# Q and K: the rounded and the remaining part of a projection, made by ScalarE and GpSimd in place of ScalarE and VectorE

## The chip, the core and the metric

The kernel runs on one core of one Trainium2 chip. The metric is the device time of one launch in microseconds (us); of the kernel before it is 1079.29 us, the median of 3 runs (1078.25 to 1079.56). TensorE multiplies, VectorE, ScalarE and GpSimd do elementwise work, SyncE issues the transfers. In the profile they are PE (PEld is its weight load), DVE, ACT, POOL and SP.

## What is computed

One transformer layer, post-LayerNorm, on 16 sequences of 512 tokens with 256 features, all in float32. 16 heads of 16 features attend in blocks of 128 tokens to the block before, their own and the block after; the feed-forward part has weights that are quantised to -1, 0 and 1.

```python
qkv = (x @ Wqkv + bqkv)                  # split into q, k, v; 16 heads of 16
scores = einsum(q_block, k_window) / 16  # window of 3 blocks, |kpos - qpos| <= 128
attn = softmax(scores)
x = layernorm(x + (attn @ v) @ Wout + bout)
h = relu(x @ quantise(W1).T + b1)
x = layernorm(x + h @ quantise(W2).T + b2)
```

## The kernel before

One row is one of the 16 sequences. The program is a software pipeline over rows, with a step for each row from -2 to 16. In a step, attention runs for row b, everything behind the attention (output projection, LayerNorms, feed-forward) for row b-1, and the projections of Q, K and V for row b+1. A step has four quarters v = 0 to 3, one for each quad of heads. The list `SIDE` names the side work of each quarter in order. In quarter 1 it is `("qk", 0), ("x1", 0), ("x1", 1), "nmt", "pv", ("x1", 2), "ut", ("x1", 3), "x1t", ("qk", 1), ("f1", 0)`; quarter 2 starts with `("f1", 1), "vp"`. Into this side work `WOVEN` puts 12 units per quarter of scores (L549, then an exp on ScalarE, L895) and of maximum scores (L567, then a masked row maximum on VectorE, L1061). Every engine walks the same list in its own program order and waits on semaphores.

Products are made from TensorE's rounded type fp32r. A float32 value is therefore kept as two tiles: hi is the value rounded, lo is what is left of it. Q and K of a row come as four tiles of 128x512, `QK[0]` to `QK[3]`; `("qk", 0)` makes `QK[0]` and `QK[1]`, `("qk", 1)` the other two. For each, TensorE fills a pair of the four shared PSUM banks `PG`. ScalarE then writes hi with the bias added (L919, `s_qkh`), and VectorE reads the same bank again, adds the bias and subtracts hi (L1088, `s_qkl`). After that the pair is free: the next user of the pair waits for `reader[k]`, here `s_qkl`. The same two steps on the same two engines make the parts of other products, `hid_hi` (L976) and `hid_lo` (L1147) of the feed-forward among them.

What stands around Q and K in quarter 1, by engine:

- TensorE: `("qk", 0)`, then the turned maxima (L631), `pv` (L641), `ut` on the pair that `("qk", 0)` had (two warming products L521 ahead of it, then L654, which needs ScalarE's copy `u`, L946), `x1t` (four warming products L521, then L612, which needs all four parts of `x1`), `("qk", 1)`, `f1` 0, `f1` 1 on the pair that `("qk", 1)` had, and `vp` on the pair of `f1` 0, for which `hid_lo` of `f1` 0 must be done.
- ScalarE: `qk_hi` twice, `x1` 0 and 1 (L963), `neg_maxT` (L938), `u` (L946), two exps, `x1` 2 and 3, the turned `x1` (L969), six exps, `qk_hi` twice, two exps, `hid_hi` twice.
- VectorE: row maxima throughout, `qk_lo` twice after units 0 and 1, the reciprocals and products of `ut` (L1095, L1102), the turned `x1`, `qk_lo` twice after unit 9, maxima 10 and 11, then `neg_max` (L1069 and L1072, two small instructions on 128x16 elements), then `hid_lo` twice.
- GpSimd: zeroes the masked probabilities after the exps 5 and 11 (L1285 and L1289), makes the small values of LayerNorm (L1351 to L1357), adds a bias to `x1` (L1360). It has no access to PSUM in this program; all that it reads is in SBUF.
- SyncE copies the parts into the stacked operands `SQ` and `SK` (`stack`, L449): first the four transfers of hi, then the two of lo, which wait for `s_qkl`; behind them in its queue stand the transfer of the maxima (L489) and later stacks. Stack 0 of the next row is first used by unit 0 of quarter 2.

Of the kernel before, what the change touches and what calls it, by code (L numbers as in the profile page):

```python
# [21 lines left out]
F32 = mybir.dt.float32  # L22
F32R = mybir.dt.float32r
ALU = mybir.AluOpType
ACT = mybir.ActivationFunctionType
# [197 lines left out]
def postln_layer(nc, xT, x, wqkv, bqk, bv, wout, bout, w1T, b1, w2T, b2, out):  # L223
    ctx = ExitStack()
    with ctx:
# [3 lines left out]
        def sem(name):  # L229
            return ctx.enter_context(nc.semaphore(name))  # L230
# [101 lines left out]
        s_qkf = sem("qk_full")  # L332
        s_qkh = sem("qk_hi_done")
        s_qkl = sem("qk_lo_done")
        s_vf = sem("v_full")
        s_v = sem("v_next_done")
        s_va = sem("v_aug_done")
# [77 lines left out]
        def _(sp):  # L415
# [17 lines left out]
            def stack(r, v, first):  # L433


                c, ih = v // 2, v % 2
                if not first:
                    sp.wait_ge(s_stf, 12 * (4 * r - 4 + v) + 12)
                half = slice(64 * ih, 64 * ih + 64)
                heads = slice(4 * ih, 4 * ih + 4)  # L440
                for part, done in ((0, s_qkh), (1, s_qkl)):
                    sp.wait_ge(done, 4 * r + 2 * c + 2)
                    for dst, j, terms in ((SQ, 2 * c, (0, 1, 0)), (SK, 2 * c + 1, (0, 0, 1))):
                        if first and v == 0 and dst is SK:
                            continue
                        for t in range(3):
                            if terms[t] == part:
                                rows = slice(64 * c + 16 * t, 64 * c + 16 * t + 16)
                                sp.dma_start(dst[rows, heads, :].bitcast(F32), QK[j][part][half, :].bitcast(F32)) \  # L449
                                    .then_inc(s_stk[v], 16)  # L450
# [51 lines left out]
        def _(pe):  # L502
# [117 lines left out]
            def side_work(v, step, b, dr, vq, at, passed):  # L620
# [37 lines left out]
                elif name == "qk":  # L658
# [8 lines left out]
                    def tokens(z, kc):  # L667
# [1 line left out]

                    in_halves(out, [three_terms(slice(0, S), lambda a, kc: weights(a, kc, j), tokens)  # L670
                                    for j in (2 * c, 2 * c + 1)], s_qkf, passed)
                    reader[k] = [(s_qkl, 4, 2 * c + 2, dr)]
                elif name in ("vp", "op"):
                    left, right, col = (XT, WQKV, 2 * D) if name == "vp" else (OT, WOUT, 0)
                    if first:
# [176 lines left out]
        def _(act):  # L852
# [10 lines left out]

            def first_k_stack():

                for part, done in ((0, s_qkh), (1, s_qkl)):
                    act.wait_ge(done, 2)
                    for t, term in enumerate((0, 0, 1)):
                        if term == part:
                            act.dma_start(SK[16 * t:16 * t + 16, 0:4, :].bitcast(F32),  # L870
                                          QK[1][part][LOWER, :].bitcast(F32)).then_inc(s_stk[0], 16)
# [26 lines left out]
            def side_work(v, step, b, dr, vq, at):  # L898
# [11 lines left out]
                elif name == "qk":  # L910
# [7 lines left out]
                    for i, j in enumerate((2 * c, 2 * c + 1)):  # L918
                        act.activation(QK[j][0][:, :], PG[:, 2 * k + i, :], ACT.Identity, bias=BQK[:, j:j + 1]) \  # L919
                            .then_inc(s_qkh, 1)  # L920
                    if first and c == 0:
                        first_k_stack()
                        weight_sums()
                    elif first:
                        act.wait_ge(s_b1, 64)
                        act.activation(B1R[:, :], B1RAW, ACT.Identity).then_inc(s_b1h, 1)
# [99 lines left out]
        def _(dve):  # L1026
# [48 lines left out]
            def side_work(v, step, b, dr, vq, at):  # L1075
# [4 lines left out]
                if step == ("xs", 1) and first:  # L1080
                    dve.wait_ge(s_xh, 2)
                    dve.tensor_tensor(XT[1][:, :, :], XRAW[:, :, :], XT[0][:, :, :].bitcast(F32),
                                      ALU.subtract).then_inc(s_xl, 1)
                elif name == "qk":
                    c = step[1]
                    for i, j in enumerate((2 * c, 2 * c + 1)):
                        dve.wait_ge(s_qkh, 4 * r + j + 1)
                        dve.scalar_tensor_tensor(QK[j][1][:, :], PG[:, 2 * k + i, :], BQK[:, j:j + 1],  # L1088
                                                 QK[j][0][:, :].bitcast(F32), ALU.add, ALU.subtract) \
                            .then_inc(s_qkl, 1)  # L1090
                elif name == "ut":
                    q = 4 * r + vq
                    dve.wait_ge(s_utf, 2 * q + 2)
# [162 lines left out]
        def _(pool):  # L1256
# [76 lines left out]
            def side_work(v, step, b, dr, vq, at):  # L1333
                name = name_of(step)
                r = b + dr
                first = at is not None and at + dr == 0
                if step == ("xs", 1) and not first:
                    pool.wait_ge(s_xh, 2 * r + 2)
                    pool.tensor_tensor(XT[1][:, :, :], XRAW[:, :, :], XT[0][:, :, :].bitcast(F32),
                                       ALU.subtract).then_inc(s_xl, 1)  # L1340
                elif name == "xr":
                    pool.wait_ge(s_xr, 16 * r + 16)
                    if first:
                        pool.wait_ge(s_b2, 32)
                    pool.tensor_tensor(Y[:, :, :], Y[:, :, :], BOUT[:, None, :].to_broadcast([P, TB, D]),
                                       ALU.add).then_inc(s_xrb, 1)
                elif name == "ln1" and step[1] % 2 == 1:
                    hf = step[1] // 2
                    two = slice(2 * hf, 2 * hf + 2)
                    pool.wait_ge(s_mv1, 4 * r + 2 * hf + 2)  # L1350
                    pool.tensor_scalar(VE[:, two], MV1[:, two, 1], 1.0, EPS, ALU.mult, ALU.add).then_inc(s_ve, 1)  # L1351
                    pool.tensor_scalar(NEG1[:, two], MV1[:, two, 0], -1.0, None, ALU.mult).then_inc(s_neg, 1)
                    pool.wait_ge(s_ve, 4 * r + 1 + hf)
                    pool.tensor_tensor(RS1[:, two], VE[:, two], HALF[:, two], ALU.pow).then_inc(s_rs1, 1)
                    pool.wait_ge(s_neg, 2 * r + hf + 1)
                    pool.wait_ge(s_rs1, 2 * r + hf + 1)
                    pool.tensor_tensor(NMR1[:, two], NEG1[:, two], RS1[:, two], ALU.mult).then_inc(s_nmr, 1)  # L1357
                elif name == "x1t":
                    pool.wait_ge(s_x1tf, 2 * r + 2)
                    pool.tensor_tensor(X1[:, :, :], X1[:, :, :], B2[:, None, :].to_broadcast([P, TB, D]),  # L1360
                                       ALU.add).then_inc(s_x1b, 1)
                elif name == "ln2" and step[1] % 2 == 1:
                    h = step[1] // 2
                    two = slice(h, h + 3, 2)
                    pool.wait_ge(s_mv2, 4 * r + 2 * h + 2)
                    pool.tensor_scalar(VE[:, two], MV2[:, two, 1], 1.0, EPS, ALU.mult, ALU.add).then_inc(s_ve, 1)
                    pool.wait_ge(s_ve, 4 * r + 3 + h)
                    pool.tensor_tensor(RS2[:, two], VE[:, two], HALF[:, two], ALU.pow).then_inc(s_rs2, 1)
                    pool.wait_ge(s_rs2, 2 * r + h + 1)
                    for t in (h, h + 2):  # L1370
                        pool.tensor_scalar(X1[:, t, :], X1[:, t, :], MV2[:, t, 0:1], RS2[:, t:t + 1],  # L1371
                                           ALU.subtract, ALU.mult).then_inc(s_o, 1)
# [82 lines left out]
```

## Time and profile before

| | kernel before |
|---|---|
| median of 3 runs | 1079.29 us (1078.25 to 1079.56) |
| the profiled execution: time | 1080.47 us |
| its span | 1078.7 us |
| PE busy | 996.8 us (92%) |
| DVE busy | 845.2 us (78%) |
| ACT busy | 620.2 us (57%) |
| POOL busy | 570.2 us (53%) |
| mean granted clock of TensorE | 0.969 of full |

The span is the profiled stretch from the first to the last instruction. The time of the same execution is 1.8 us longer, the launch around it. A busy share is an average over the whole span; what a step costs is read from the timeline of a row, where one sees which wait ends last. A wait is printed in square brackets behind the instruction that it held up, with the engine that ended it.

### The profile page before, as it was taken

Reading aid. Unit: us, or ns where it says so; the run is one execution under the profiler, and the core shown is the slowest. Engines: PE = TensorE matmul, PEld = TensorE weight load, DVE = VectorE, ACT = ScalarE, POOL = GpSimd, SP = SyncE. Lnnn points to the kernel's source line nnn. Section 1 sums busy time; section 2 is a strip of 40 time slices with the busy share of each in tenths; the row PEclk is TensorE's granted clock in tenths of the full one; section 3 lists DMA queues with packets and bytes.
Section 4 is the critical chain, followed back from the end, with each engine's and each line's share of the span. In section 5 each row is a group of like instructions: output and inputs, shape, how many; then the busy total and the mean of one; then the engine's idle time right before and its main releaser. Section 6 shows DMA issues by size and latency. Waiting matters only on the chain.

```text
span 1078.7 us, 29877 instructions
## 1 busy us (share of the span) xinstructions
PE 996.8 (92%) x11270; PEld 782.0 (72%) x11270; DVE 845.2 (78%) x2966; ACT 620.2 (57%) x1273; POOL 570.2 (53%) x913
## 2 busy tenths in 40 slices
PE   6898999999999999999999999999999999999897
PEld 5675777777777777777767777786777778687677
DVE  3775888879788887978888787988878798887535
ACT  4244665746566574756657474765747475564632
POOL 3975356374655537465554646454464645445352
PEclk8577999999999999999999999999999999999999
DMA  9554336546354545626454652645365364435000
GB/s 222 64 82 72 57 57 95 81 74 94 55 91 66 96 70 81 99 43 97 66 96 63 94 87 49 100 65 96 56 100 80 57 96 68 73 52 81 22 21 20
DMA packets 57023, 81.90 MB, mean 76 GB/s; under 512 B 7712, under 2 KB 27696, under 8 KB 56880
## 3 DMA queue, kind: packets, MB, share of 16 engines
q1 hardware_dynamic: 56640, 79.60, 46.8%
q8 instruction: 90, 1.47, 0.7%
q10 hardware_dynamic: 240, 0.39, 0.3%
q14 instruction: 53, 0.43, 0.2%
HBM read 20.20 MB, written 8.39 MB: 26 GB/s over the span
## 4 chain that ended last, share of the span: by engine, by line
PE 61%; DVE 13%; ACT 12%; issue 6%; POOL 4%; DMA 2%; SPq 1%; DVEq 0%; POOLq 0%; ACTq 0%
PE shared L592 26%; PE shared L641 11%; PE st L549 8%; PE mx L567 6%; DVE mx L1061 6%; ACT probs L895 4%; PE shared L521 2%; ACT x L963 2%; ACT u L946 2%; DVE hid_lo L1147 2%; PE shared L654 2%; ACT oT_x1T_hi L969 2%; PE shared L612 1%; POOL probs L1285 1%; POOL probs L1289 1%
## 5 line engine op out<-in xcount | busy, mean ns | idle before, releaser
L1061 DVE CUSTOM_DVE_ANT_0 mx<-mx,band 128x384 f32<-128x384 f32 (+1 forms) x1024 | 478.9, 518 | 150.5 <-PE mx L567 145.4
L895 ACT ACTIVATE probs<-st 128x384 f32<-128x384 f32 (+1 forms) x768 | 365.1, 526 | 169.8 <-PE st L549 168.1
L1285 POOL TENSOR_SCALAR_AFFINE_SELECT probs<-probs 128x512 f32<-128x512 f32 (+1 forms) x256 | 127.8, 524 | 407.0 <-ACT probs L895 407.0
L567 PE MATMUL mx<-k_stack,q_stack 48*128 48x384 f32 (+1 forms) x1024 | 271.7, 347 | 8.5 <-DMA q_stack<-qk_lo 4.9
L549 PE MATMUL st<-q_stack,k_stack 50*128 50x384 f32 (+1 forms) x1024 | 245.1, 334 | 7.8 <-ACT probs L895 3.8
L549 PEld LDWEIGHTS st<-q_stack,k_stack 50*128 50x128 f32 x1024 | 167.7, 189 | 58.9 <-issue 29.8
L567 PEld LDWEIGHTS mx<-k_stack,q_stack 48*128 48x128 f32 x1024 | 171.8, 193 | 31.1 <-DVE rmax L1061 19.2
L641 PE MATMUL shared<-probs,v_aug 128*32 128x384 f32 (+1 forms) x2048 | 164.2, 444 | 9.4 <-POOL probs L1289 7.2
L1061 DVE DVE_READ_ACCUMULATOR2_ANT rmax<- 128x1 f32 x1024 | 144.9, 141 | 0.0
L592 PE MATMUL shared<-w2q,hid_hi 64*128 64x256 f32 x960 | 137.0, 289 | 0.0
L641 PEld LDWEIGHTS shared<-probs,v_aug 128*32 128x32 f32 x2048 | 90.5, 111 | 55.8 <-issue 17.7
L592 PE MATMUL shared<-w2q,hid_lo 64*128 64x256 f32 x960 | 129.2, 278 | 0.0
L1289 POOL TENSOR_SCALAR_AFFINE_SELECT probs<-probs 128x512 f32<-128x512 f32 (+1 forms) x256 | 127.7, 523 | 0.0
L592 PEld LDWEIGHTS shared<-w2q,hid_lo 64*128 64x128 f32 x960 | 114.9, 185 | 0.0
L592 PEld LDWEIGHTS shared<-w2q,hid_hi 64*128 64x128 f32 x960 | 113.3, 185 | 0.4
L592 PE MATMUL shared<-oT_x1T_hi,w1q 64*128 64x512 f32 x480 | 104.0, 398 | 0.0
L592 PE MATMUL shared<-oT_x1T_lo,w1q 64*128 64x512 f32 x480 | 102.4, 394 | 0.0
L946 ACT ACTIVATE u<-shared 128x512 f32<-128x512 f32 x64 | 37.9, 593 | 102.1 <-PE shared L641 102.0
L521 PE MATMUL shared<-wqkv_hi 64*128 64x512 f32 x516 | 86.6, 417 | 3.9 <-DVE qk_lo L1088 3.8
L1147 DVE SCALAR_TENSOR_TENSOR hid_lo<-shared,hid_hi 128x512 fp32r<-128x512 f32 x120 | 77.0, 682 | 16.1 <-ACT hid_hi L976 16.1
L1371 POOL TENSOR_SCALAR x<-x,ln_mv,ln_rstd 128x256 f32<-128x256 f32 x60 | 73.5, 1230 | 3.2
L976 ACT ACTIVATE hid_hi<-shared 128x512 fp32r<-128x512 f32 x120 | 65.2, 596 | 13.9 <-PE shared L592 12.7
(165 smaller groups left out, 1935.7 us busy)
## 6 DMA issues: line engine op xcount, KB each, us to landing
q_stack<-qk_hi SPq DMA_DIRECT2D x128, 128.0 KB, 4.0
k_stack<-qk_hi SPq DMA_DIRECT2D x126, 128.0 KB, 4.9
x_raw<-in_xT SPq DMA_DIRECT2D x16, 512.0 KB, 6.0
q_stack<-qk_lo SPq DMA_DIRECT2D x64, 128.0 KB, 5.6
y<-in_x SPq DMA_DIRECT2D x16, 512.0 KB, 6.3
out<-x SPq DMA_DIRECT2D x32, 256.0 KB, 2.4
k_stack<-qk_lo SPq DMA_DIRECT2D x63, 128.0 KB, 5.8
probs<-in_w2T SPq DMA_DIRECT2D x1, 1024.0 KB, 7.5
```

What stands on the lines that cost most here:

```text
L521: pe.matmul(out[i][:, 0:width], WQKV[0][rows, 0, 0:P], WQKV[0][rows, 1, 0:width], start=True, stop=True)
L549: mm = pe.matmul(PST[i % N_SCORE][:, col:col + n], SK[rows, hd, W * m:W * m + W], SQ[rows, hd, q0:q0 + n], start=True, stop=True)
L567: mm = pe.matmul(PMX[i % N_MAX][:, col:col + n], SQ[rows, hd, W * m:W * m + W], SK[rows, hd, k0:k0 + n], start=True, stop=True)
L592: mm = pe.matmul(out[k][:, cols], lhs(rows), rhs(rows), start=(swap == 0 and n == 0 and bias is None), stop=(swap == 1 and n == count - 1) ...
L641: mm = pe.matmul(out[0][32 * g:32 * g + 32, q0:q0 + width], VAUG[:, vq, m, g, :], PR[:, vq % 2, g // 2, lo:lo + width], start=(m == 0), st ...
L895: act.activation(PR[:, v % 2, g // 2, lo:lo + n], PST[i % N_SCORE][:, 0:n], ACT.Exp, scale=SCALE) \
L976: act.activation(HID[0][:, f, :], PG[:, 2 * k + i, :], ACT.Relu).then_inc(s_hh, 1)
L1061: mx = dve.tensor_tensor_reduce(ps, ps, band, 1.0, -3e38, ALU.add, ALU.max, RMAX[:, g, m:m + 1])
L1147: dve.scalar_tensor_tensor(HID[1][:, f, :], PG[:, 2 * k + i, :], 0.0, HID[0][:, f, :].bitcast(F32), ALU.max, ALU.subtract).then_inc(s_hl, 1)
L1285: pool.affine_select(out=pr_before, in_=pr_before, compare_op=ALU.is_ge, fill=0.0, base=0, pattern=[[0, n], [1, W]], channel_multiplier=-1)
L1289: last = pool.affine_select(out=pr_after, in_=pr_after, compare_op=ALU.is_ge, fill=0.0, base=0, pattern=[[0, n], [-1, W]], channel_multipl ...
L1371: pool.tensor_scalar(X1[:, t, :], X1[:, t, :], MV2[:, t, 0:1], RS2[:, t:t + 1], ALU.subtract, ALU.mult).then_inc(s_o, 1)
```

## The change

For every row but the first, ScalarE copies each bank of Q and K twice. The first copy is hi as before. The second writes the full value with its bias into the lo tile, as plain float32 (`s_qkw`, new). GpSimd then subtracts hi from it in place, SBUF to SBUF, and raises `s_qkl`. VectorE no longer touches Q and K of these rows. The pair of banks is free when ScalarE's second copies are done. The first row keeps the old way, with a semaphore of its own (`s_qkl0`). On GpSimd the new step stands behind the masks that are woven into the `qk` step; in quarter 1 that is ahead of the mask of exp 11.

```diff
--- before.py
+++ after.py
@@ -332,6 +332,8 @@
         s_qkf = sem("qk_full")
         s_qkh = sem("qk_hi_done")
         s_qkl = sem("qk_lo_done")
+        s_qkl0 = sem("qk_lo_done_in_first_row")
+        s_qkw = sem("qk_copied")
         s_vf = sem("v_full")
         s_v = sem("v_next_done")
         s_va = sem("v_aug_done")
@@ -438,8 +440,13 @@
                     sp.wait_ge(s_stf, 12 * (4 * r - 4 + v) + 12)
                 half = slice(64 * ih, 64 * ih + 64)
                 heads = slice(4 * ih, 4 * ih + 4)
-                for part, done in ((0, s_qkh), (1, s_qkl)):
-                    sp.wait_ge(done, 4 * r + 2 * c + 2)
+                for part in range(2):
+                    if part == 0:
+                        sp.wait_ge(s_qkh, 4 * r + 2 * c + 2)
+                    elif first:
+                        sp.wait_ge(s_qkl0, 2 * c + 2)
+                    else:
+                        sp.wait_ge(s_qkl, 4 * r - 4 + 2 * c + 2)
                     for dst, j, terms in ((SQ, 2 * c, (0, 1, 0)), (SK, 2 * c + 1, (0, 0, 1))):
                         if first and v == 0 and dst is SK:
                             continue
@@ -669,7 +676,7 @@
 
                     in_halves(out, [three_terms(slice(0, S), lambda a, kc: weights(a, kc, j), tokens)
                                     for j in (2 * c, 2 * c + 1)], s_qkf, passed)
-                    reader[k] = [(s_qkl, 4, 2 * c + 2, dr)]
+                    reader[k] = [(s_qkl0, 0, 2 * c + 2, dr)] if first else [(s_qkw, 4, 2 * c - 2, dr)]
                 elif name in ("vp", "op"):
                     left, right, col = (XT, WQKV, 2 * D) if name == "vp" else (OT, WOUT, 0)
                     if first:
@@ -863,7 +870,7 @@
 
             def first_k_stack():
 
-                for part, done in ((0, s_qkh), (1, s_qkl)):
+                for part, done in ((0, s_qkh), (1, s_qkl0)):
                     act.wait_ge(done, 2)
                     for t, term in enumerate((0, 0, 1)):
                         if term == part:
@@ -918,6 +925,9 @@
                     for i, j in enumerate((2 * c, 2 * c + 1)):
                         act.activation(QK[j][0][:, :], PG[:, 2 * k + i, :], ACT.Identity, bias=BQK[:, j:j + 1]) \
                             .then_inc(s_qkh, 1)
+                        if not first:
+                            act.activation(QK[j][1][:, :].bitcast(F32), PG[:, 2 * k + i, :], ACT.Identity,
+                                           bias=BQK[:, j:j + 1]).then_inc(s_qkw, 1)
                     if first and c == 0:
                         first_k_stack()
                         weight_sums()
@@ -1081,13 +1091,13 @@
                     dve.wait_ge(s_xh, 2)
                     dve.tensor_tensor(XT[1][:, :, :], XRAW[:, :, :], XT[0][:, :, :].bitcast(F32),
                                       ALU.subtract).then_inc(s_xl, 1)
-                elif name == "qk":
+                elif name == "qk" and first:
                     c = step[1]
                     for i, j in enumerate((2 * c, 2 * c + 1)):
                         dve.wait_ge(s_qkh, 4 * r + j + 1)
                         dve.scalar_tensor_tensor(QK[j][1][:, :], PG[:, 2 * k + i, :], BQK[:, j:j + 1],
                                                  QK[j][0][:, :].bitcast(F32), ALU.add, ALU.subtract) \
-                            .then_inc(s_qkl, 1)
+                            .then_inc(s_qkl0, 1)
                 elif name == "ut":
                     q = 4 * r + vq
                     dve.wait_ge(s_utf, 2 * q + 2)
@@ -1338,6 +1348,11 @@
                     pool.wait_ge(s_xh, 2 * r + 2)
                     pool.tensor_tensor(XT[1][:, :, :], XRAW[:, :, :], XT[0][:, :, :].bitcast(F32),
                                        ALU.subtract).then_inc(s_xl, 1)
+                elif name == "qk" and not first:
+                    for j in (2 * step[1], 2 * step[1] + 1):
+                        pool.wait_ge(s_qkw, 4 * r - 4 + j + 1)
+                        pool.tensor_tensor(QK[j][1][:, :], QK[j][1][:, :].bitcast(F32), QK[j][0][:, :].bitcast(F32),
+                                           ALU.subtract).then_inc(s_qkl, 1)
                 elif name == "xr":
                     pool.wait_ge(s_xr, 16 * r + 16)
                     if first:
```

## Rows read from the trace of the kernel before

**Rows 1.** The page: busy time by engine; then the chain that ended last.
```profile
PE 996.8 (92%) x11270; PEld 782.0 (72%) x11270; DVE 845.2 (78%) x2966; ACT 620.2 (57%) x1273; POOL 570.2 (53%) x913
PE 61%; DVE 13%; ACT 12%; issue 6%; POOL 4%; DMA 2%; SPq 1%; DVEq 0%; POOLq 0%; ACTq 0%
```
**Rows 2.** Windows: stretch, its length, busy PE PEld DVE ACT POOL, clock, DMA.
```profile
40.00:80.00 40.00, 35.81 (x216) 26.09 (x218) 28.68 (x109) 16.67 (x35) 33.17 (x37) 0.68 0.72 93
...
120.00:182.40 62.40, 58.88 (x708) 46.29 (x706) 51.71 (x184) 38.29 (x80) 33.33 (x55) 1.00 0.48 71
...
931.20:993.60 62.40, 58.84 (x710) 46.38 (x708) 51.88 (x185) 37.26 (x79) 30.95 (x54) 1.00 0.46 71
```
**Rows 3.** Timeline of ScalarE from 436 us: start, length, line, operands, count, [idle <-releaser].
```profile
435.86 1.27 ACT L919 ACTIVATE qk_hi<-shared,bqk 128x512 fp32r<-128x512 f32 x2 [0.79 <-PE shared L592]
437.49 1.09 ACT L963 ACTIVATE x<-y,ln_neg_mean_rstd,ln_rstd 128x256 f32<-128x256 f32 x2 [0.36 <-POOL ln_neg_mean_rstd L1357]
...
439.97 1.07 ACT L963 ACTIVATE x<-y,ln_neg_mean_rstd,ln_rstd 128x256 f32<-128x256 f32 x2
```
**Rows 4.** Timeline of TensorE in the same stretch, instructions that waited.
```profile
439.27 0.51 PE L521 MATMUL shared<-wqkv_hi 64*128 64x512 f32 x2 [0.37 <-DVE qk_lo L1088]
...
441.10 0.28 PE L612 MATMUL shared<-identity,x 64*128 64x64 f32 x2 [0.21 <-ACT x L963]
```
**Rows 5.** Timeline of VectorE in the same stretch.
```profile
437.81 1.41 DVE L1088 SCALAR_TENSOR_TENSOR qk_lo<-shared,bqk,qk_hi 128x512 fp32r<-128x512 f32 x2
```
**Rows 6.** Timeline of ScalarE around the second Q and K step.
```profile
446.65 1.27 ACT L919 ACTIVATE qk_hi<-shared,bqk 128x512 fp32r<-128x512 f32 x2
447.80 1.00 ACT L895 ACTIVATE probs<-st 128x384 f32<-128x384 f32 x2
448.96 1.09 ACT L976 ACTIVATE hid_hi<-shared 128x512 fp32r<-128x512 f32 x2 [0.17 <-PE shared L592]
```
**Rows 7.** Timeline of VectorE around the second Q and K step.
```profile
448.71 0.56 DVE L1061 CUSTOM_DVE_ANT_0 mx<-mx,band 128x384 f32<-128x384 f32 x1
...
450.12 0.36 DVE L1069 TENSOR_SCALAR neg_max<-rmax 128x16 fp32r<-128x16 f32 x1
450.51 0.32 DVE L1072 SCALAR_TENSOR_TENSOR neg_max<-rmax,neg_max 128x16 f32<-128x16 f32 x1
450.76 1.27 DVE L1147 SCALAR_TENSOR_TENSOR hid_lo<-shared,hid_hi 128x512 fp32r<-128x512 f32 x2
```
**Rows 8.** Timeline of TensorE's weight loads there, those that waited.
```profile
448.84 0.18 PEld L579 LDWEIGHTS shared<-ones,b_rows 64*128 64x128 f32 x2 [0.39 <-DVE qk_lo L1088]
452.09 0.19 PEld L592 LDWEIGHTS shared<-wqkv_hi,xT_hi 64*128 64x128 f32 x2 [0.97 <-DVE hid_lo L1147]
```
**Rows 9.** Timeline of GpSimd in quarter 1.
```profile
438.85 0.20 POOL L1357 TENSOR_TENSOR ln_neg_mean_rstd<-ln_neg_mean,ln_rstd 128x2 f32<-128x2 f32 x1
...
446.10 2.39 POOL L1360 TENSOR_TENSOR x<-x,b_rep 128x1024 f32<-128x1024 f32 x1
448.87 1.00 POOL L1285 TENSOR_SCALAR_AFFINE_SELECT probs<-probs 128x512 f32<-128x512 f32 x2 [0.38 <-ACT probs L895]
```
**Rows 10.** Timeline of GpSimd beside the neg_max pair of Rows 7.
```profile
450.40 0.41 POOL L1289 TENSOR_SCALAR_AFFINE_SELECT probs<-probs 128x256 f32<-128x256 f32 x1
```
**Rows 11.** The first neg_max of the run, and GpSimd beside it.
```profile
35.67 1.27 POOL L1303 TENSOR_TENSOR w2q<-w2q,oT_x1T_lo 128x512 fp32r<-128x512 f32 x1
36.93 1.56 POOL L1299 TENSOR_SCALAR oT_x1T_lo<-probs,abs_sums_thresholds 128x512 fp32r<-128x512 f32 x1
36.26 0.71 DVE L1069 TENSOR_SCALAR neg_max<-rmax 128x16 fp32r<-128x16 f32 x1
37.01 0.63 DVE L1072 SCALAR_TENSOR_TENSOR neg_max<-rmax,neg_max 128x16 f32<-128x16 f32 x1
```
**Rows 12.** Timeline of SyncE, stack 0; then the page's DMA issues (median us to landing).
```profile
440.36 0.61 SPq L449 DMA_DIRECT2D k_stack<-qk_lo  x1
...
k_stack<-qk_lo SPq DMA_DIRECT2D x63, 128.0 KB, 5.8
```

## The prediction

> **What bounds the kernel now.** I read the page first: TensorE is busy 92% of the span, VectorE 78%, ScalarE 57%, GpSimd 53%, but the chain that ended last is only 61% TensorE; 13% of it is VectorE and 12% ScalarE [rows 1]. So TensorE sets the pace with handovers in between, and what the change is worth depends on who ends which handover, not on the shares. The windows show 14 rows alike from 120 to 993.6 us: 62.4 us each, of which TensorE is busy 58.8 to 58.9, at a granted clock of 1.00, that is the 2.4 GHz level [rows 2]. The change touches quarter 1 of every row, so the timeline of one such row (the step from 432 us) decides, and 14 times its shift is the answer.
>
> In that quarter there are two places. In the first (436 to 441 us) ScalarE works almost without a gap: `qk_hi` twice, 0.36 us of waiting, then `x1`, `neg_maxT`, `u`, exps, `x1` to 441.04 [rows 3]; TensorE then waits for the last `x1`, until 441.10 [rows 4]. Its wait for `qk_lo` just before (0.37 us [rows 4]) is followed by warming products and is not the last handover. In the second place VectorE works in one piece from 448.71 to 452.03: maxima 10 and 11, `neg_max`, `hid_lo` [rows 7], and TensorE's next projection waits for that `hid_lo` until 452.09, its weight load for 0.97 us; shortly before, it waited 0.39 us for `qk_lo` [rows 8].
>
> **The change, part by part.** It removes 2 VectorE instructions per step, 1.41 us as a pair [rows 5], and adds 2 ScalarE copies and 2 GpSimd subtractions. Over 30 steps (15 rows, 2 each) VectorE loses 42 us of work.
>
> A ScalarE copy: two `qk_hi` take 446.65 to 447.80, where the next instruction starts [rows 6], so 0.575 us each in a sequence. Between there and the whole 0.69 of the last one (1.27 less 0.575 [rows 3]) I take 0.575, because neighbours overlap in the same way here. Two more: +1.15 us.
>
> The Trainium skill ("ScalarE: Activation LUTs", What ACT_TABLE_LOAD costs) gives an ACTIVATE with a bias operand 280 ns + 0.833 ns per element less about 93 ns of overlap, an estimate of 0.614 us for 512 elements; the two would be 1.23 us. The row is shorter and decides.
>
> First place. Four copies run from 435.86 to 438.16 and `x1` 0 starts there, not at 437.49 [rows 3]: +0.67. GpSimd's LayerNorm values were ready by 437.49, so ScalarE itself is late next. All that stands behind `x1` 0 in its queue follows: `u`, two exps, and the last `x1`, whose end moves from 441.04 to 441.71. The pair of banks is free at about 438.4 instead of 439.2, but then `ut` waits for `u`, and TensorE's wait for the last `x1` still ends last. Shift of TensorE behind this place: +0.67. VectorE's 1.41 us buy nothing here.
>
> GpSimd in the first place: it is free at 439.05, and until 446.10 it has one mask to do, four instructions in some 2 us [rows 9]. Two subtractions of 128x512, bounded by the 1.27 us of a subtraction of that size [rows 11] and half of the 2.39 us of 1024 columns, 1.20 [rows 9]; I take 1.27, the same size: 439.05 to 441.6. The lo transfers of stack 0, the later of which was issued at 440.36 and takes 5.8 us to land [rows 12], go at about 442.3 and land at 448.1; their first user stands just behind the first half of `f1` 1, at about 451. Behind them in SyncE's queue the transfer of the maxima moves from about 441.0 to 442.9, for the same user. Cost nothing; the cover is 3 us.
>
> Second place. ScalarE arrives 0.67 late (447.32), makes four copies (to 449.62), then the two exps (1.16 to the next start, less the 0.17 of waiting [rows 6]: 0.99, to 450.61), then `hid_hi`, whose first half ends at about 451.2 and whose second at 451.70. `hid_lo` could then run 451.25 to 452.5. TensorE gets the pair for `f1` 1 at 449.85 instead of 448.84 (+1.01), and comes to the projection at 451.12 (452.09 less 0.97 [rows 8]) + 1.01 = 452.13, ahead of 452.5. By ScalarE alone the projection starts at 452.6: +0.5 a row.
>
> But VectorE has `neg_max` ahead of `hid_lo`, and there GpSimd matters. The two small instructions take 0.36 and 0.32 us at 450.12 and 450.51 [rows 7]. The second ends at 450.83, GpSimd's mask instruction beside it at 450.81 [rows 10]. At the start of the run L1069 takes 0.71, from 36.26 to 36.97, while a GpSimd subtraction of 128x512 ends at 36.94; the instruction after it, L1072, takes 0.63 beside a GpSimd instruction with one tensor input, and ends before it [rows 11]. I read this as: while a GpSimd instruction runs, at least one that subtracts, `neg_max` waits for its end.
>
> The Trainium skill ("SBUF — State Buffer", Who interferes with whom) says that a VectorE instruction in a 2-port mode, or with two SBUF inputs while GpSimd reads SBUF, and a GpSimd instruction exclude each other for a whole instruction. By that rule, which speaks against this change, the trace mostly agrees; the 0.63 us of L1072 it does not explain.
>
> In the changed kernel GpSimd ends the bias of `x1` (446.10 + 2.39 [rows 9]) 0.67 later, at 449.16, and its subtractions run 449.16 to 450.43 and, the second copy of `QK[3]` being done at 449.73, 450.39 to 451.66. Maxima 10 and 11 no longer stand behind `qk_lo` but behind TensorE; they start at about 448.4 and `neg_max` is issued at about 449.85. Its first half then ends with the first subtraction (450.46), its second with the second (451.7), and `hid_lo` runs to about 452.89 in place of 452.03: +0.86 a row. The mask of exp 11 goes from 448.87 [rows 9] to 451.7; its `pv` comes ten us later, so this is free.
>
> **The sum.** 14 rows x 0.86 = 12.0 us. The fifteenth row (63 to 76 us) has no LayerNorm or feed-forward beside it and lies where the clock is 0.68 [rows 2]; I take 0, with 1 us either way. The profiled execution of 1080.47 would become 1092.5; it lies 1.2 above the median, so the median becomes 1091.3. Bounds: a shift of 0.6 to 1.3 a row (0.575 to 0.69 for a copy at four places, and one subtraction more or less beside `neg_max`) gives 1087.7 to 1097.5.
>
> **Rivals.** (A) The forecast, 1091.3. (B) VectorE isn't held by GpSimd, or `neg_max` falls beside only one subtraction: +0.5 a row, 7.0 us, 1086.3. For it: one subtraction is all that the trace shows holding it. (C) The other side, faster: ScalarE's copies hide and VectorE's relief counts. The place is the start of the projection. With no delay on ScalarE `hid_lo` would follow `hid_hi` (448.96 + 1.09 = 450.05) and end at 451.3; the projection would start 0.74 earlier, 14 x 0.74 = 10.4 us, 1068.9. It decides once ScalarE's `x1` no longer waits for its own copies, that is with 1.15 us of gap in the first place; the row shows 0.36. (D) The delays are taken up by waits further on: nothing within 0.2% (2.2 us). Against it: TensorE waits nowhere else for something that doesn't itself follow TensorE. (E) More than a wait: TensorE idles longer in each row and the granted clock drops to 1.2 GHz in some stretch, as before 120 us (0.68 [rows 2]). With 5 us a row at half speed: 14 x 2.5 = 35 us, 1126.
>
> **How the numbers follow.** A 0.48, B 0.27, C 0.07, D 0.09, E 0.09. The range 1080 to 1098 holds A with its bounds, B and about half of D, and leaves out C, E and the rest, about 0.2. A difference of 0.2% is about what can be told from no change here. Faster 0.07, same 0.09, slower 0.84.
>
> **What would show it.** In the changed profile: four activations in a row at each `qk` step, 2.3 us to the next start; `x1` 0 directly behind them without idle time; L1069 and L1072 of quarter 1 (0.36 and 0.32 now) ending with the GpSimd subtractions, L1072 above 1 us; the projection waiting for `hid_lo` longer than 0.97; VectorE's busy time lower by 42 us less what `neg_max` gains in waiting; rows 0.5 to 0.9 us longer. Wrong would be: idle time of ScalarE ahead of `x1` (then C or D), waits of TensorE for `q_stack` or `k_stack` in quarter 2 (late transfers, a cost that I set at nothing), or a clock below 1.00 after 120 us.

## The result, and the profile after

| | before | after |
|---|---|---|
| median | 1078.77 us (4 runs, 1077.79 to 1079.56) | 1094.57 us (4 runs, 1092.76 to 1096.6) |
| ratio | 1 | 1.0128 (95% interval 1.0107 to 1.015) |
| profiled execution: time, span | 1080.47, 1078.7 us | 1093.96, 1092.0 us |

The change makes the kernel 1.3% slower by the ratio on record; the two medians lie 15.8 us apart, which is 1.5%, and the spans of the two profiled executions 13.3 us. The forecast was 12.0 us (1091.3), the range 1080 to 1098. The lines that answer to [rows 1], from the page of the changed kernel:

```profile
PE 997.7 (91%) x11270; PEld 780.0 (71%) x11270; DVE 825.4 (76%) x2906; ACT 649.5 (59%) x1333; POOL 642.4 (59%) x973
...
PE 68%; ACT 12%; DVE 9%; issue 5%; POOL 3%; DMA 2%; SPq 1%; POOLq 0%; ACTq 0%; DVEq 0%
```

VectorE has 60 instructions fewer but only 19.8 us less busy time, not 42: all `neg_max` instructions together take 55.6 us in place of 40.1, which is 15.5 of the 22 us between. ScalarE and GpSimd are busy 29 and 72 us more. The shares of the page would not tell that the kernel has become slower.

A row can be timed by any instruction that comes back once in it. Here it is one of the four copies of the turned maxima that ScalarE makes in a row, the one that has waited 1.22 us, on the timeline of the changed kernel:

```profile
161.17 0.27 ACT L948 ACTIVATE neg_maxT<-shared 32x128 fp32r<-32x128 f32 x1 [1.22 <-PE shared L638]
...
224.30 0.27 ACT L948 ACTIVATE neg_maxT<-shared 32x128 fp32r<-32x128 f32 x1 [1.21 <-PE shared L638]
```

and of the kernel before:

```profile
158.81 0.27 ACT L938 ACTIVATE neg_maxT<-shared 32x128 fp32r<-32x128 f32 x1 [1.22 <-PE shared L631]
...
221.19 0.27 ACT L938 ACTIVATE neg_maxT<-shared 32x128 fp32r<-32x128 f32 x1 [1.22 <-PE shared L631]
```

Over all full rows the usual distance (the median of the 14) is 62.34 us before and 63.14 after: +0.80 us a row, forecast +0.86. That is 14 x 0.80 = 11.2 us.

**The first place.** ScalarE in the changed kernel (it answers to [rows 3]):

```profile
441.45 0.69 ACT L926 ACTIVATE qk_hi<-shared,bqk 128x512 fp32r<-128x512 f32 x1 [0.79 <-PE shared L599]
442.03 0.68 ACT L929 ACTIVATE qk_lo<-shared,bqk 128x512 f32<-128x512 f32 x1
442.60 0.69 ACT L926 ACTIVATE qk_hi<-shared,bqk 128x512 fp32r<-128x512 f32 x1
443.17 0.70 ACT L929 ACTIVATE qk_lo<-shared,bqk 128x512 f32<-128x512 f32 x1
443.74 1.10 ACT L973 ACTIVATE x<-y,ln_neg_mean_rstd,ln_rstd 128x256 f32<-128x256 f32 x2
...
446.21 1.07 ACT L973 ACTIVATE x<-y,ln_neg_mean_rstd,ln_rstd 128x256 f32<-128x256 f32 x2
```

Four activations in 2.29 us, 0.573 each, and `x1` behind them without idle time. From the start of the first copy to that of the last `x1` pair it is 4.76 us; in [rows 3] it is 4.11. So the place costs 0.65, forecast 0.67. TensorE's waits (they answer to [rows 4]):

```profile
445.51 0.46 PE L661 MATMUL shared<-identity,u 64*128 64x64 f32 x8 [0.77 <-ACT u L956]
446.84 0.28 PE L619 MATMUL shared<-identity,x 64*128 64x64 f32 x2 [0.24 <-ACT x L973]
447.33 0.28 PE L619 MATMUL shared<-identity,x 64*128 64x64 f32 x2 [0.21 <-ACT x L973]
```

In this row the wait for `qk_lo` is gone, and one for `u`, twice as long, has taken its place: ScalarE, which frees the banks sooner, delivers everything else later.

**The second place.** VectorE and, beside it, GpSimd (they answer to [rows 7] and [rows 9]):

```profile
455.49 0.51 DVE L1079 TENSOR_SCALAR neg_max<-rmax 128x16 fp32r<-128x16 f32 x1
456.03 1.22 DVE L1082 SCALAR_TENSOR_TENSOR neg_max<-rmax,neg_max 128x16 f32<-128x16 f32 x1
457.17 1.28 DVE L1157 SCALAR_TENSOR_TENSOR hid_lo<-shared,hid_hi 128x512 fp32r<-128x512 f32 x2
```
```profile
454.69 2.52 POOL L1354 TENSOR_TENSOR qk_lo<-qk_lo,qk_hi 128x512 fp32r<-128x512 f32 x2
457.17 0.99 POOL L1295 TENSOR_SCALAR_AFFINE_SELECT probs<-probs 128x512 f32<-128x512 f32 x2
```

Two instructions on 16 columns take 0.51 and 1.22 us, in place of 0.36 and 0.32. The first ends at 456.00, when GpSimd's first subtraction does (454.69 and half of 2.52, 455.95 to 455.97); the second ends at 457.25, 0.04 after the second subtraction (457.21). `hid_lo` ends at 458.45, and TensorE's projection starts right after:

```profile
458.50 0.39 PE L599 MATMUL shared<-wqkv_hi,xT_hi 64*128 64x256 f32 x2 [0.41 <-DVE hid_lo L1157]
```

The Trainium skill ("SBUF — State Buffer", Who interferes with whom) says that VectorE and GpSimd exclude each other for a whole instruction when VectorE's has two SBUF inputs or runs in a 2-port mode. L1082, with two inputs, agrees: 1.22 us, to the end of the subtraction. L1079, with one, is held as well; whether it runs in a 2-port mode no view here shows.

The weight loads of TensorE that waited there (they answer to [rows 8]):

```profile
455.37 0.19 PEld L586 LDWEIGHTS shared<-ones,b_rows 64*128 64x128 f32 x2 [0.64 <-ACT qk_lo L929]
458.50 0.18 PEld L599 LDWEIGHTS shared<-wqkv_hi,xT_hi 64*128 64x128 f32 x2 [0.85 <-DVE hid_lo L1157]
```

The pair for `f1` 1 comes from ScalarE's last copy and comes later, not sooner. The wait for `hid_lo` is 0.85 us, shorter than the 0.97 before, since TensorE itself arrives later.

### The profile page after: what moved, and what is told of

Its sections match the earlier page's. It is cut to its first block, busy times and chain, and to the rows that moved or that the text cites. A ratio compares the mean times of both kernels' runs of the same rounds, so it can differ in the third digit from the quotient of the medians.

```text
span 1092.0 us, 29937 instructions
## 1 busy us (share of the span) xinstructions
PE 997.7 (91%) x11270; PEld 780.0 (71%) x11270; DVE 825.4 (76%) x2906; ACT 649.5 (59%) x1333; POOL 642.4 (59%) x973
## 4 chain that ended last, share of the span: by engine, by line
PE 68%; ACT 12%; DVE 9%; issue 5%; POOL 3%; DMA 2%; SPq 1%; POOLq 0%; ACTq 0%; DVEq 0%
PE shared L599 32%; PE shared L648 11%; PE st L556 9%; PE mx L574 7%; DVE mx L1071 4%; ACT probs L902 4%; PE shared L528 3%; ACT x L973 2%; ACT u L956 2%; PE shared L661 2%; DVE neg_max L1082 2%; PE shared L619 1%; ACT oT_x1T_hi L979 1%; POOL probs L1295 1%; POOL probs L1299 1%
## 5 line engine op out<-in xcount | busy, mean ns | idle before, releaser
L599 PE MATMUL shared<-w2q,hid_hi 64*128 64x256 f32 x960 | 136.8, 289 | 0.0
L599 PE MATMUL shared<-w2q,hid_lo 64*128 64x256 f32 x960 | 128.9, 278 | 0.0
L599 PEld LDWEIGHTS shared<-w2q,hid_lo 64*128 64x128 f32 x960 | 114.1, 185 | 0.0
L599 PEld LDWEIGHTS shared<-w2q,hid_hi 64*128 64x128 f32 x960 | 112.6, 185 | 0.5
L599 PE MATMUL shared<-oT_x1T_hi,w1q 64*128 64x512 f32 x480 | 103.5, 398 | 0.0
L599 PE MATMUL shared<-oT_x1T_lo,w1q 64*128 64x512 f32 x480 | 101.8, 394 | 0.0
L1354 POOL TENSOR_TENSOR qk_lo<-qk_lo,qk_hi 128x512 fp32r<-128x512 f32 x60 | 75.6, 1283 | 2.0 <-ACT qk_lo L929 2.0
```

The lines of the kernel that those rows point to most:

```text
L599: mm = pe.matmul(out[k][:, cols], lhs(rows), rhs(rows), start=(swap == 0 and n == 0 and bias is None), stop=(swap == 1 and n == count - 1) ...
L1354: pool.tensor_tensor(QK[j][1][:, :], QK[j][1][:, :].bitcast(F32), QK[j][0][:, :].bitcast(F32), ALU.subtract).then_inc(s_qkl, 1)
```

## The experiments

Theory 1 is the forecast's: ScalarE delays the first place, GpSimd's subtractions hold VectorE's `neg_max` in the second. Rivals: GpSimd holds nothing and ScalarE is the whole cost; or the gain of VectorE pays some of it back. The results stand together below. In the table a row is the distance that the shortest full rows share, all at a granted clock of 1.00; in the two kernels above it is the median too, while in some below about half of the rows are longer. "At half clock" is the time at the 1.2 GHz level, worked out from the mean granted clock c of all executions as 2 x (1 - c) x time:

| kernel | ratio to before (95% interval) | row, us | at half clock, us (before beside it) |
|---|---|---|---|
| changed kernel, again | 1.015 (1.0126 to 1.0174) | 63.13 | 74.5 (65.0) |
| changed, `neg_max` late | 1.0215 (1.019 to 1.0239) | 63.6 | 82.7 (65.0) |
| before, `neg_max` late | 0.995 (0.9933 to 0.9966) | 61.9 | 64.9 (65.0) |
| before, more GpSimd work | 1.0088 (1.0059 to 1.0116) | 63.08 | 62.6 (65.0) |
| first step only | 1.0094 (1.0063 to 1.0125) | 62.98 | 73.1 (65.6) |
| second step only | 1.002 (1.0003 to 1.0037) | 62.50 | 65.6 (65.6) |
| ScalarE twice, VectorE too | 1.0268 (1.0237 to 1.0298) | 64.1 to 64.4 | 79.9 (65.6) |
| half copy | 1.0043 (1.002 to 1.0065) | 62.72 | 64.5 (65.6) |
| changed, GpSimd behind the mask | 1.0091 (1.0057 to 1.0125) | 62.72 | 82.3 (66.7) |
| second step only, behind the mask | 0.9961 (0.9945 to 0.9978) | 62.06 | 66.7 (66.7) |
| before, `neg_max` late, again | 0.9949 (0.9932 to 0.9966) | 61.92 | 67.0 (66.7) |
| changed, one input on GpSimd | one execution, 1089.91 us | 62.72 | 80.7 (66.7) |

**The changed kernel once more.**

> The changed kernel once more, beside the others. Both theories: 14 to 16 us above the kernel before, as measured; a row takes 63.14 us in place of 62.34, so 14 x 0.80 = 11.2 us lie in the rows and 3 to 4 us are still to be found, in the start or in the clock.

The shortest rows are the same, 63.1 us, but three took 64.1 to 64.4, two 63.6 and one 63.8. What these are is told below, under the clock.

**More GpSimd work alone.** The suspected cause without the rest of the change. A semaphore, `s_again`, which ScalarE waits for before it reads the tile in the next row, keeps the values safe; its other lines are left out here:

```diff
+                elif step == ("qk", 1) and not first and stages(at)[3]:
+                    pool.wait_ge(s_x, 16 * (r + 1) + 16)
+                    for kc in range(KC):
+                        pool.tensor_tensor(XRAW[:, kc, :], XRAW[:, kc, :], ONES_R[:, :].bitcast(F32), ALU.mult).then_inc(s_again, 1)
...
```

> The kernel before, with two GpSimd products of 128x512 (by one, in place, on the next row's raw x) where the changed kernel has its subtractions of the second Q and K step; ScalarE and VectorE do what they did. In 13 full rows. Theory 1: they run 448.5 to 451.0, neg_max (issued at 450.12) waits for the second one and then for the first mask instruction, to about 451.65 in place of 450.83, so 0.84 us a row, 13 x 0.84 = 10.9 us, about 1.010. Rival: GpSimd's work is hidden and its mask has time; no change beyond 1 us.

A row takes 63.08 us, +0.74 (expected +0.84), and the last full row, which has not got the two products, 62.34 as before. VectorE and GpSimd in it:

```profile
454.96 0.87 DVE L1072 TENSOR_SCALAR neg_max<-rmax 128x16 fp32r<-128x16 f32 x1
455.86 0.55 DVE L1075 SCALAR_TENSOR_TENSOR neg_max<-rmax,neg_max 128x16 f32<-128x16 f32 x1
```
```profile
454.51 1.29 POOL L1347 TENSOR_TENSOR x_raw<-x_raw,ones 128x512 f32<-128x512 f32 x1
455.75 0.64 POOL L1288 TENSOR_SCALAR_AFFINE_SELECT probs<-probs 128x512 f32<-128x512 f32 x1
```

The ends meet again, 455.83 with 455.80 and 456.41 with 456.39. ScalarE reads the tile some 14 us after the products, so nobody waits for this work, and it costs 0.7 us a row by where it lies: the rival that GpSimd holds nothing falls.

**GpSimd behind the mask.** In the changed kernel, the subtractions of the second step moved from ahead of the mask of exp 11 to behind it:

```diff
-                elif name == "qk" and not first:
-                    for j in (2 * step[1], 2 * step[1] + 1):
+                elif step in (("qk", 0), ("f1", 0)):
+                    r = b + 1
+                    for j in ((0, 1) if step == ("qk", 0) else (2, 3)):
```

> The changed kernel with GpSimd's two subtractions of the second Q and K step behind the mask of exp 11 in place of ahead of it. Theory 1: at the time of neg_max GpSimd then waits for exp 11 (which ends about 0.2 us later), so neg_max takes 0.17 us twice; hid_lo follows hid_hi and a row is 0.4 us shorter than in the changed kernel: a period of 62.74 in place of 63.14, 5.6 us, about 1.008 of the kernel before. That is ScalarE's share alone (0.40 a row over the 62.34 of the kernel before); in the run with neg_max issued late, row maxima of quarter 2 had taken the gain back. Rival: GpSimd's place doesn't matter, 63.14 as in the changed kernel.

```profile
449.43 0.17 DVE L1079 TENSOR_SCALAR neg_max<-rmax 128x16 fp32r<-128x16 f32 x1
449.64 0.18 DVE L1082 SCALAR_TENSOR_TENSOR neg_max<-rmax,neg_max 128x16 f32<-128x16 f32 x1
450.68 0.69 DVE L1157 SCALAR_TENSOR_TENSOR hid_lo<-shared,hid_hi 128x512 fp32r<-128x512 f32 x1 [0.87 <-ACT hid_hi L986]
```

`neg_max` is free, and VectorE waits 0.87 us for ScalarE. A row takes 62.72 us. So of the 0.80 us, 0.42 is GpSimd's hold of VectorE, and 0.38 is what ScalarE's copies cost over what VectorE's relief gives back. The time of the run (1.0091, 9.7 us) is less good than 14 x 0.38 = 5.3 us would make it; it is one of the runs with more time at half clock, and three of its rows are longer, 63.5 to 63.6 us, at a lower clock.

**The late `neg_max`, in both kernels.** VectorE's two small instructions of quarter 1 behind `hid_lo`:

```diff
-                                if what == UNITS - 1:
+                                if what == UNITS - 1 and v != 1:
                                     neg_max(b + q[0], q[1], at == -1)
...
+                    if v == 1 and q is not None:
+                        neg_max(b + q[0], q[1], at == -1)
```

> The changed kernel with neg_max of quarter 1 issued behind hid_lo in place of ahead of it. Theory 1 (VectorE is held in neg_max by GpSimd's two subtractions, 0.51 and 1.22 us in place of 0.17 each): hid_lo no longer stands behind it and follows hid_hi, which ends at 457.16 of the row in which hid_lo now ends at 458.45; hid_lo would end at about 458.05, 0.4 us a row earlier, 14 x 0.4 = 5.6 us less than the changed kernel, about 1.008 of the kernel before. Rival (ScalarE's copies alone hold the second place, GpSimd doesn't hold VectorE): hid_lo is bound by hid_hi anyway and nothing changes beyond 1 us.

> The kernel before with neg_max of quarter 1 issued behind hid_lo in place of ahead of it. Theory 1: maxima 10 and 11 end at 450.08, hid_hi at 450.05, so hid_lo runs 450.1 to 451.4 in place of 450.76 to 452.03 and TensorE, which is there at 451.12, goes on at 451.45 in place of 452.09: 0.64 us a row, 9 us less than the kernel before, about 0.992. Rival (the wait for hid_lo is not the one that counts, another ends with it): under 2 us.

In the kernel before it gains 0.41 us a row, less than the 0.64 expected but clear: 0.995. In the changed kernel it loses 0.46 where I had expected 0.4 of gain. Its VectorE:

```profile
461.10 0.27 DVE L1079 TENSOR_SCALAR neg_max<-rmax 128x16 fp32r<-128x16 f32 x1
461.40 0.55 DVE L1082 SCALAR_TENSOR_TENSOR neg_max<-rmax,neg_max 128x16 f32<-128x16 f32 x1
461.98 0.57 DVE L1071 CUSTOM_DVE_ANT_0 mx<-mx,band 128x384 f32<-128x384 f32 x1
```

the masks on GpSimd beside the first two:

```profile
460.93 0.40 POOL L1297 TENSOR_SCALAR_AFFINE_SELECT probs<-probs 128x256 f32<-128x256 f32 x1
461.29 0.63 POOL L1301 TENSOR_SCALAR_AFFINE_SELECT probs<-probs 128x512 f32<-128x512 f32 x1
```

and the waits of TensorE's weight loads in it:

```profile
461.23 0.19 PEld L599 LDWEIGHTS shared<-wqkv_hi,xT_hi 64*128 64x128 f32 x2 [0.40 <-DVE hid_lo L1157]
465.10 0.18 PEld L574 LDWEIGHTS mx<-k_stack,q_stack 48*128 48x128 f32 x1 [0.51 <-DVE rmax L1071]
```

The part of the expectation on `hid_lo` is right (from TensorE's start on `f1` 1 to its start on the projection it is 2.68 us there, 3.12 in the changed kernel). But now the masks hold `neg_max`, for 0.27 and 0.55 (to 461.37 and 461.95, 0.04 and 0.03 after the two masks), and behind it stand the row maxima of quarter 2, for which TensorE waits at 465.10. From the start of that projection to TensorE's next feed-forward product (L586) it is 4.73 us in place of 3.83: 0.90 lost behind it and 0.44 gained ahead of it make the 0.46. I had moved a held instruction and not asked what is queued behind it in its new place. In the kernel before the masks are done by then, and it takes 0.17 and 0.18.

**One step of the two alone.** The other step stays with VectorE reading the banks:

```diff
-                        if not first:
+                        if not first and c == 0:      # or c == 1
                             act.activation(QK[j][1][:, :].bitcast(F32), PG[:, 2 * k + i, :], ACT.Identity,
...
-                elif name == "qk" and first:
+                elif name == "qk" and (first or step[1] != 0):
```

> The change for the first Q and K step of a row alone; the second stays as in the kernel before. Theory 1: ScalarE's 1.15 us less its gap of 0.36 and what overlaps make the last part of x1 0.67 us late, and everything behind it, VectorE's piece of work in the second place too: 14 x 0.67 = 9.4 us, about 1.009. Rival 1 (the delay is taken up by the time that VectorE has gained): under 3 us. Rival 2 (costs simply add, with the other half alone): see there.

> The change for the second Q and K step of a row alone. Theory 1: ScalarE's two copies end at 448.95, hid_hi at 451.03; GpSimd's subtractions run 448.5 to 451.0 and hold neg_max until then; hid_lo ends at about 452.3 in place of 452.03: 14 x 0.25 = 3.5 us, about 1.003. With the first step alone at 9.4 the sum would be 12.9, in both together 11.2 in the rows. Rival (GpSimd holds nothing; ScalarE alone): hid_lo is bound by hid_hi, about the same end, so this run alone doesn't tell; it tells how much of the whole lies in which step.

Rows of +0.64 and +0.16 us, against 0.67 and 0.25 expected. Their sum is the 0.80 of both together. Four fifths of the loss is the first step, which saves VectorE 1.41 us where nothing critical waited for it.

**The second step with GpSimd behind the mask.** The two findings put together:

> The change for the second Q and K step alone, with GpSimd's subtractions behind the mask of exp 11. Theory 1: the first place stays as before; in the second neg_max is free at about 449.5, hid_hi ends at 451.03 and hid_lo at 451.75 in place of 452.03, so a row is 0.2 to 0.3 us shorter than in the kernel before: a period of about 62.1, 3.4 us, 0.997. That would be a form of the change that gains. Rival (ScalarE's 1.15 us are never paid back): 62.5 as without the move, 1.002.

VectorE in it:

```profile
449.69 0.69 DVE L1159 SCALAR_TENSOR_TENSOR hid_lo<-shared,hid_hi 128x512 fp32r<-128x512 f32 x1 [0.87 <-ACT hid_hi L988]
```

A row takes 62.06 us, 0.28 less than before, and the ratio is 0.9961 (0.9945 to 0.9978). In this form and at this place the change gains. VectorE has `neg_max` behind it (0.17 and 0.18 us) ahead of the masks, and `hid_lo` waits for ScalarE alone. From the start of `qk_hi` to the end of the first two `hid_lo` it is 5.11 us, in place of 5.38 before ([rows 6], [rows 7]).

**ScalarE twice, VectorE as well.** ScalarE's copies without VectorE's relief and without GpSimd:

```diff
                         dve.wait_ge(s_qkh, 4 * r + j + 1)
+                        if not first:
+                            dve.wait_ge(s_qkw, 4 * r - 4 + j + 1)
```

> ScalarE makes the full copies as in the changed kernel, but VectorE still makes lo from the banks as in the kernel before (over the copy, and only once the copy is there); GpSimd does nothing new. Theory 1: the first place costs 0.67 as before; in the second VectorE has qk_lo ahead of maxima 10 and 11 again and it starts later, so hid_lo ends 1.4 to 2.0 us late: 14 x 1.4 to 2.0 = 20 to 28 us, 1.018 to 1.026. So VectorE's relief is worth 0.6 to 1.2 us a row, once ScalarE is loaded. Rival (VectorE's relief is worth nothing): as the changed kernel, 1.013.

TensorE in it, at the start of `f1` 1:

```profile
851.66 0.50 PE L580 MATMUL shared<-ones,b_rows 64*128 64x512 f32 x2 [1.09 <-DVE qk_lo L1094]
```

Rows of 64.1 to 64.4 us at a clock of 1.00, +1.8 to +2.1, at the upper end of the 1.4 to 2.0 expected; six more took 64.9 to 65.2 at a lower clock, and the whole, 30.1 us and 1.0268, lies just above the 1.018 to 1.026 expected. The changed kernel has +0.80, so once ScalarE has its copies, taking the subtraction off VectorE is worth about 1.0 us a row. TensorE's waits show where: for the pair of `f1` 1 it waits 14.1 us in 14 rows for `qk_lo`, in the changed kernel 2.7 in 13 for ScalarE's copy. Some of this is VectorE's wait for the copy, which only this kernel has.

**Half a copy.** The second halves of the lo tiles are left without their full value:

```diff
-                            act.activation(QK[j][1][:, :].bitcast(F32), PG[:, 2 * k + i, :], ACT.Identity,
+                            act.activation(QK[j][1][:, 0:S // 2].bitcast(F32), PG[:, 2 * k + i, 0:S // 2], ACT.Identity,
```

> The changed kernel with ScalarE's second copies cut to 256 of the 512 columns; the second halves of the lo tiles of Q and K are left without their full value, GpSimd subtracts all 512 as before. Theory 1: a copy takes 0.36 us in place of 0.575 in a sequence, two copies 0.43 less; x1 is late by 0.24 in place of 0.67. GpSimd's subtractions move 0.43 earlier with the row and neg_max stays behind them: a row is 0.43 us shorter than in the changed kernel, 6 us, about 1.007. Rival (the price is the number of activations or the wait for GpSimd, not ScalarE's length): no change beyond 1 us.

Rows of 62.72 us, 0.42 less than in the changed kernel, 0.43 expected: the price goes with ScalarE's length. The time, 1.0043, is better than the 1.007 expected; this kernel hasn't the extra time at half clock either.

**One input on GpSimd.** One execution, profiled. The lo tiles of `QK[2]` and `QK[3]` hold half the full value here:

```diff
+                            pool.tensor_scalar(QK[j][1][:, :], QK[j][1][:, :].bitcast(F32), 0.5, None,
+                                               ALU.mult).then_inc(s_qkl, 1)
```

> The changed kernel with GpSimd's two instructions of the second Q and K step as a product with a constant, one tensor input in place of two (lo of QK[2] and QK[3] is left as half the full value). It asks which GpSimd instructions hold neg_max. Theory 1a (any that reads SBUF): L1079 and L1082 of the changed kernel's lines end 0.02 to 0.04 us after the two instructions. Theory 1b (only those with two tensor inputs, and the masks): neg_max takes 0.17 us twice and the row about 62.7 us. At the start of the kernel before, L1072 took 0.63 us beside a product-like GpSimd instruction and ended before it, which speaks for something between.

```profile
451.37 2.96 POOL L1358 TENSOR_SCALAR qk_lo<-qk_lo 128x512 fp32r<-128x512 f32 x2
```
```profile
452.13 0.17 DVE L1079 TENSOR_SCALAR neg_max<-rmax 128x16 fp32r<-128x16 f32 x1
452.34 0.18 DVE L1082 SCALAR_TENSOR_TENSOR neg_max<-rmax,neg_max 128x16 f32<-128x16 f32 x1
```

`neg_max` lies within GpSimd's products with a constant and is not held; so it is in 9 of the 14 full rows. In the other five the clock was lower, and L1082 took 0.52 to 0.54 us. The shortest rows are 62.72 us, as with GpSimd behind the mask.

**The `neg_max` move once more.**

> The kernel before with neg_max of quarter 1 behind hid_lo once more, in more rounds: 61.93 us a row in place of 62.34, about 6 us, 0.995. No theory of the change hangs on it; it says whether this version beats both kernels.

0.9949 (0.9932 to 0.9966), 1074.87 us: it beats both kernels. The second step behind the mask, measured beside it, has 1076.66 us. Whether the two gains add was not tried.

**The clock.** Some times are longer than 14 usual rows make them. The windows of the second run of the changed kernel (the columns are those of [rows 2]) show a long row, from the first place on:

```profile
317.60:320.60 3.00, 2.21 (x29) 1.36 (x24) 1.95 (x9) 3.00 (x8) 2.86 (x4) 1.00 0.65 122
320.60:323.60 3.00, 2.57 (x24) 2.25 (x26) 1.91 (x8) 1.64 (x5) 0.45 (x1) 0.70 1.02 110
323.60:326.60 3.00, 3.00 (x24) 2.50 (x23) 2.02 (x6) 1.85 (x5) 1.95 (x5) 0.73 0.43 47
```

TensorE is busy 2.21 of 3 us there, then its granted clock averages 0.70 and 0.73, so that for some 3.4 of 6 us it is at the 1.2 GHz level (0.30 and 0.27 of 3 us, doubled), and the row takes 64.1 us in place of 63.1. The next row, 64.12 us on, is nearly the same up to there, keeps its clock, and takes 63.1:

```profile
381.72:384.72 3.00, 2.19 (x29) 1.36 (x24) 1.97 (x9) 3.00 (x8) 2.86 (x4) 1.00 0.62 120
384.72:387.72 3.00, 2.59 (x30) 1.96 (x30) 1.91 (x8) 1.90 (x5) 0.43 (x1) 1.00 1.05 114
```

In a corresponding stretch of the kernel before TensorE is busy more, and the clock stays at 1.00:

```profile
438.20:441.20 3.00, 2.41 (x31) 1.71 (x30) 2.91 (x11) 2.84 (x7) 0.71 (x2) 1.00 0.90 145
```

The profiled executions tell the kernels apart. In those with the whole delay of ScalarE in the first place the clock fell right behind that place in 1 of 14 rows (the changed kernel, first time), 4 (second time), 4 (`neg_max` late), 3 (first step only), 4 (behind the mask), 5 (one input) and 6 (ScalarE twice). In the other seven, the one with half a copy among them, it fell there in none. The one drop of the changed kernel's first profile is this:

```profile
130.00:133.00 3.00, 2.72 (x26) 2.32 (x28) 1.91 (x8) 1.72 (x5) 0.31 (x1) 0.70 1.12 126
```

The last column of the table agrees in the mean, 7 to 18 us more at half clock with the whole delay and none more without, though single executions of one kernel differ by up to 25 us. TensorE's busy time ahead does not single out the rows: in the 3 us that begin 2.3 us behind the start of the first `qk_hi` it is about 2.36 us with ScalarE twice and the clock fell in six rows, with half a copy 2.37 and it fell in none. What picks the row stays open. The three long rows of the second run took 1.0 to 1.2 us more, about 1.1 for each 3.4 us at half clock, so the 9.5 us more of that run cost about 3 us (an estimate).

## Why the prediction was right

**What bounds, and where to look.** Right. The two places named are the two that moved, and their two shares (0.64 and 0.16 us) make up the whole 0.80 of a row. One sign in the list was wrong by the prediction's own sum: it asks for a wait for `hid_lo` above 0.97 us, while TensorE at 452.13 and `hid_lo` at 452.89 leave about 0.8; measured, 0.85.

**The first place.** 0.575 us a copy was 0.573, +0.67 was 0.65 in the trace and 0.64 a row in the run with this step alone. The wait for `u` came as told.

**GpSimd's subtractions.** 1.27 us was 1.28. They cost nothing in the first place, and TensorE has no new wait for a late transfer in the rows: the two for transfers of `qk_lo` on its list, 5.6 us at 25 us and 0.8 us at 50, belong to the start and were 4.9 and 0.8 before.

**The second place.** `neg_max` took 0.51 and 1.22 us where I had 0.6 and 1.2, `hid_lo` followed it, and +0.86 was +0.80. The split was 0.5 by ScalarE and 0.36 by GpSimd's hold; the run with GpSimd behind the mask shows 0.38 and 0.42. By steps, 0.67 of the 0.86 came from the first and 0.19 from the second; the two runs show 0.64 and 0.16.

**The sum.** 14 x 0.80 = 11.2 against 12.0 us. In the two profiled executions the 13.3 us can be followed: 0.7 us are lost by 93 us, 1.7 from there to 161 us, 10.2 in the next 13 rows, 0.8 behind them. The 1.7 are a row's 0.80 and 0.9 more, where the clock fell to 0.70 at 130 us. The prediction had named a clock below 1.00 after 120 us as a sign of being wrong, and it is there. The 0.7 at the start is the size of the longer transfer wait at 25 us and lies within the 1 us that it allowed there. The 0.8 behind the rows it did not price, and their cause is not shown.

The medians differ by 15.8. The term that was mis-sized is rival E, the clock, which I had priced as all or nothing (35 us, chance 0.09) and left out of the sum. It came in part, in some rows of some executions, beside the forecast and not in its place. With it the second run adds up to 11.2 + 3 = 14 of 16.1 us. The rest, about 2 us, stays open. Part of it goes with the rows of 63.6 us. Their extra 0.4 us arise on TensorE, 25 us into the row, in its products of `x` and `wqkv` (L599), with no wait listed and a clock of 1.00; the cause isn't found. So the mechanism of the forecast came as told, but that the median lies only 3.3 us above it owes something to the price of the clock being small.

**Rivals.** B (VectorE not held) falls with the two GpSimd runs, C and D with every run that has the first step. The place from which C should decide did decide: ScalarE's lack of a gap ahead of `x1`. At the second place ScalarE has no gap for its copies either, but with `neg_max` free VectorE waits for ScalarE and still ends `hid_lo` earlier than before, and the change gains 0.28 us a row.

## What to carry to other kernels

Before work is taken off an engine, ask for each place by itself who waits for that engine there: of two equal moves in one row, one saved time that nothing critical had waited for and cost 0.64 us, and the other, with GpSimd out of the way, gained 0.28. Work for GpSimd has a price that stands in no wait list of GpSimd: look which short VectorE instructions with operands in SBUF will lie beside it, and what is queued behind them. And where an engine falls a little further behind TensorE, look at TensorE's granted clock over all executions, not only at the row.

## What the runs showed of the hardware

- A VectorE instruction on 128x16 elements in SBUF took up to 1.32 us (0.17 when free) beside GpSimd subtractions and products of two tensors, and in the rows shown ended 0.02 to 0.05 us after them. Beside the masks (TENSOR_SCALAR_AFFINE_SELECT, one tensor input) it was held too, for 0.27 to 0.55 us. Beside a GpSimd product with a constant, 1.5 us for 128x512, it took 0.17 and 0.18 and was not. The rule of the Trainium skill ("SBUF — State Buffer", Who interferes with whom) is that a VectorE instruction with two SBUF inputs contends with any GpSimd instruction that reads SBUF; the last run does not bear that out.
- TensorE's granted clock fell to the 1.2 GHz level in single full rows, at one place: in 27 of 98 rows of the seven profiled executions with the whole delay of ScalarE, in none of 98 of the seven others. In the rows shown TensorE had been busy 2.21 of 3 us ahead of the drop, and 2.19 of 3 us where none followed. Between whole and half copies of ScalarE the difference is 0.4 us of delay a row.
